# Moving two statistics chains ahead of the weight reloads in GpSimd's program

## The reference

```python
xn = layernorm(x)                       # over the last axis, eps 1e-5
a  = tanh(xn @ Wa.T + ba)               # (8, 4096, 64)
b  = tanh(xn @ Wb.T + bb)
h[t] = a[t] * h[t-1] + b[t]             # scan over the 4096 tokens
attn = xn + h @ Wout.T + bout
scale = mean(abs(weight))               # weight is 2048 x 2048
w_t = clip(round(weight / (scale + 1e-10)), -1, 1)
ffn = xn @ (w_t * scale).T + bias
y = x + attn + ffn
```

## Time and profile before

| what | us |
|---|---|
| median of the timed runs (758.03 to 758.31) | 758.17 |
| the profiled execution's own time | 758.21 |
| span of its slowest core (core 0) | 756.6 |
| spans of its eight cores | 752.0 to 756.6 |
| mean granted TensorE clock of the cores | 0.992 to 0.995 |

### The profile page before, as it was taken

One profiled execution on the slowest core, in us unless ns is written; L12 is line 12 of the kernel. 1 busy time (PEld: TensorE's weight loads), 2 busy tenths in 40 slices (PEclk: granted clock), 3 DMA queues, 4 the chain that ended last, 5 costly groups with the idle time before them and its releaser, 6 DMA issues.

```text
span 756.6 us, 11239 instructions; the slowest of 8 cores (752.0 to 756.6 us)
## 1 busy us (share of the span) xinstructions
PE 586.7 (78%) x3740; PEld 310.8 (41%) x3804; DVE 349.0 (46%) x303; ACT 235.7 (31%) x250; POOL 217.3 (29%) x742
## 2 busy tenths in 40 slices
PE   0111314404799999999999999999999999999995
PEld 0110213303444454444444454444444444544442
DVE  0000099841354455544556545555445555455521
ACT  0664414504422332233222223322332222232220
POOL 0000012265033333333333334333333333333410
PEclk9999999999899999999999999999999999999998
DMA  7998128840132233233433333333343333233222
GB/s 228 340 331 270 28 106 252 263 158 1 56 112 112 112 112 112 112 131 121 160 146 113 112 112 112 112 112 113 128 161 137 131 112 113 112 112 112 112 84 83
DMA packets 16831, 103.02 MB, mean 136 GB/s; under 512 B 4326, under 2 KB 4358, under 8 KB 4358
## 3 DMA queue, kind: packets, MB, share of 16 engines
q1 hardware_dynamic: 9350, 51.96, 21.2%
q0 software_dynamic: 7424, 50.34, 17.4%
HBM read 68.73 MB, written 33.55 MB: 135 GB/s over the span
## 4 chain that ended last, share of the span: by engine, by line
PE 64%; DMA 10%; ACT 8%; issue 4%; ACTq 4%; DVEq 4%; DVE 3%; POOL 1%; POOLq 1%; SPq 1%
PE pffn L560 15%; PE pffn L546 15%; PE pffn L556 14%; PE pffn L543 13%; DMA vv<-wf 8%; ACT xnT L302 4%; ACTq L301 3%; PE pab L534 2%; PE ptr L570 2%; DVE wbn L368 2%; DVEq L362 2%; ACT xnT L298 1%; DVEq L367 1%; DMA outb<-wf 1%; POOL wocv L612 1%
## 5 line engine op out<-in xcount | busy, mean ns | idle before, releaser
L560 PE MATMUL pffn<-w_rhs,xnT 128*128 128x512 bf16 x512 | 195.1, 381 | 3.3 <-ACT w_rhs L259 1.7
L546 PE MATMUL pffn<-w_rhs,xnT 128*128 128x512 bf16 x496 | 188.0, 379 | 1.6
L556 PE MATMUL pffn<-w_rhs,xnT 128*128 128x512 bf16 x480 | 182.9, 381 | 0.0
L543 PE MATMUL pffn<-w_rhs,xnT 128*128 128x512 bf16 x465 | 176.2, 379 | 0.0
L346 DVE TENSOR_REDUCE sums<-sx 128x1 f32<-128x2048 f32 x32 | 73.2, 2286 | 140.4 <-DMA sx<-x 140.1
L298 ACT COPY xnT<-ptr 128x1024 bf16<-128x1024 bf16 x31 | 31.4, 1012 | 243.2 <-PE ptr L570 243.2
L397 DVE SCALAR_TENSOR_TENSOR outb<-pffn,negs,vv 128x1024 f32<-128x1024 f32 x32 | 41.1, 1284 | 117.7 <-PE pffn L586 102.5
L280 ACT ACTIVATE xnb<-sx,nmr,yr 128x2048 bf16<-128x2048 f32 x31 | 65.0, 2096 | 96.3 <-POOLq L657 96.2
L623 POOL TENSOR_SCALAR mm_<-sums 128x1 f32<-128x1 f32 x32 | 7.2, 226 | 249.9 <-DVE sqscr L348 246.8
L480 PE MATMUL ptr<-sidn,wbn 128*128 128x128 bf16 x256 | 28.5, 296 | 65.1 <-DVE wbn L368 37.6
L556 PEld LDWEIGHTS pffn<-w_rhs,xnT 128*128 128x128 bf16 x512 | 50.3, 98 | 62.5 <-issue 2.9
(11 more groups left out here) (109 smaller groups left out, 607.3 us busy)
## 6 DMA issues: line engine op xcount, KB each, us to landing
sx<-x SPq DMA_DIRECT2D x32, 1024.0 KB, 5.2
y<-outb POOLq DMA_DIRECT2D x32, 1024.0 KB, 5.7
outb<-wf POOLq DMA_DIRECT2D x11, 1024.0 KB, 7.3
wtile<-wf SPq DMA_DIRECT2D x8, 1024.0 KB, 11.0
vv<-wf SPq DMA_DIRECT2D x8, 1024.0 KB, 13.8
sqscr<-wf POOLq DMA_DIRECT2D x5, 1024.0 KB, 6.4
wasb<-wa SPq DMA_DIRECT2D x1, 512.0 KB
wosb<-wout SPq DMA_DIRECT2D x1, 512.0 KB, 18.1
```

Of the source, the lines that this page charges most:

```text
L543: tensor.matmul(pffn[:, 0:512], lhs, w_rhs[:, 2048 * c:2048 * c + 512], start=st_, stop=False)
L546: tensor.matmul(pffn[:, 512:1024], lhs, w_rhs[:, 2048 * c + 512:2048 * c + 1024], start=st_, stop=False)
L556: tensor.matmul(pffn[:, 1024:1536], lhs, w_rhs[:, 2048 * c + 1024:2048 * c + 1536], start=st_, stop=False)
L560: ins = tensor.matmul(pffn[:, 1536:2048], lhs, w_rhs[:, 2048 * c + 1536:2048 * c + 2048], start=st_, stop=False)
```

## The change

Only the order in POOL's program changes. The sixteen weight reloads and the sixteen wocv DMAs, which stood ahead of `chain(0)` and `chain(1)`, now stand behind both, directly ahead of POOL's loop over the token tiles. No instruction is added, removed or altered, and no other engine's program changes.

```diff
             g.memset(two_i[:, :], 2)
-            for j in range(NW):
-                if j < 3:
-                    g.wait_ge(s_wabs, 10 + 2 * j)
-                    if j == 2:
-                        g.wait_ge(s_sums, 2)
-                else:
-                    g.wait_ge(s_tern, j - 2)
-                sl = j % 3
-                buf = outb if sl < 2 else sqscr
-                so = (sl % 2) * D if sl < 2 else 0
-                g.dma_start(out=buf[:, so:so + D],
-                            in_=wf_d[128 * j:128 * (j + 1), :]
-                            ).then_inc(s_wlb[sl], 16)
-            g.wait_ge(s_cvecv, 1)
-            for i in range(16):
-                g.dma_start(out=wocv[64:65, 128 * i:128 * (i + 1)],
-                            in_=cneg[i:i + 1, :]).then_inc(s_cvr, 16)
-
             def chain(j):
...
             chain(0)
             chain(1)
+            for j in range(NW):
+                if j < 3:
+                    g.wait_ge(s_wabs, 10 + 2 * j)
+                    if j == 2:
+                        g.wait_ge(s_sums, 2)
+                else:
+                    g.wait_ge(s_tern, j - 2)
...
+            g.wait_ge(s_cvecv, 1)
+            for i in range(16):
...
             for k in range(NT):
```

More of the change, by code:

```diff
@@ L660, in _ @@
             chain(1)
+            for j in range(NW):
[5 more added lines that the diff above has]
+                    g.wait_ge(s_tern, j - 2)
+                sl = j % 3
+                buf = outb if sl < 2 else sqscr
+                so = (sl % 2) * D if sl < 2 else 0
+                g.dma_start(out=buf[:, so:so + D],
+                            in_=wf_d[128 * j:128 * (j + 1), :]
+                            ).then_inc(s_wlb[sl], 16)
+            g.wait_ge(s_cvecv, 1)
+            for i in range(16):
+                g.dma_start(out=wocv[64:65, 128 * i:128 * (i + 1)],
+                            in_=cneg[i:i + 1, :]).then_inc(s_cvr, 16)
             for k in range(NT):
```

## The result

The changed kernel takes 747.08 us (median of 7 runs, 746.51 to 749.34); the kernel before, timed with it, 758.0 (6 runs). The ratio is 0.986, with a 95% interval of 0.9847 to 0.9873: 10.9 us less. The forecast was 748.3 us, 9.9 us less.

A forecast was written before the change was run, and what follows sets the result against it. TensorE's steady loop is full and untouched, so the some 200 us of preparation before it decide; -6.2 (first read) and -3.7 (ternary stage to TensorE, late start included) make -9.9, 748.3 us; range 743.5 to 754.

The forecast's parts named there:

- Term 1: First read of the weight: without two early reloads in the full DMA engines, the last Abs comes 6.2 us earlier.
- Term 2: Start of the ternary stage: reloads issued behind both chains put the first comparison 19.6 us later, at 123.26.
- Term 3: First comparison to TensorE: twelve tiles keep 48.04 us, xnb fits between copies, tile 12's copies end 3.7 us earlier.
- A: Ternary stage: squaring doesn't hold POOL (-1.95) and twelve tiles take 45.7 us: -14.2, 744.0 us; chance 0.15.
- B: First three queued reloads share the queue, the first landing 12.7 us after issue instead of 6.5: 754.5 us; chance 0.17.
- C: Ternary stage bound by its three buffers' round trip; landing of 10.3 us eats the gain, 12.9 gives 768 us; chance 0.04.

The follow-up runs named there:

- run 1: The kernel before, with weight reloads 0 and 1 held back until ScalarE has cast the second small weight: 751.29 us, ratio 0.9919.
- run 7: The changed kernel, with reloads 1 and 2 each issued only when the one before has landed: 752.14 us, ratio 0.9937 to the kernel before.
- Run 4: The changed kernel, with VectorE's sums of tiles 0 and 1 heading its program and reloads 0 and 1 awaiting the second small weight's cast: 717.61 us, ratio 0.9476.
- run 3: The changed kernel, with only chain(0) ahead of the reloads and chain(1) behind the wocv DMAs: 739.74 us, ratio 0.977 to the kernel before.
- run 5: The kernel before, with reloads 0 and 1 held back, VectorE's sums at its program's head, chains still behind all reloads: 740.73 us, ratio 0.9786.
- run 2: The kernel before, with both chains moved behind reloads 0 and 1 but ahead of the other reloads: 751.69 us profiled, 753.6 in a second execution.

## Why the prediction was right

**Term 1, the first read (-6.2 us).** Right in cause and near in size: at the last Abs core 5 measured -6.8 us, the eight cores -4.6 to -7.9 with a mean of -6.4, and run 1 alone -6.1 us in the total. One step behind it was off: what follows the last Abs isn't quite a fixed sequence. The second small weight was waited for longer, and of the 6.8 us only 5.9 reached VectorE's sums.

**Term 2, the late start of the ternary stage (+19.6 us on the old clock).** Measured on core 5: the first comparison moved from 103.05 to 118.09, and with the 5.9 us by which the sums came earlier taken out that is +20.9 us. Piece by piece: semaphore to chain 0.26 us (0.56 taken), chain to chain 9.28 (7.45 + 1.95 = 9.40), chain(1) from 102.06 to 109.34 is 7.28 (7.12), to the issue 0.76 (0.70), to the comparison 7.99 us (6.5). The hold of 1.95 us, the one cost that no row had shown, was 1.86 (L620 took 2.05 us; beside an idle VectorE it takes 0.19). The one piece that was off is the landing, too short by 1.5 us on the core that became the slowest, too long by 1.1 us on the even ones. Together the pieces make +1.3 us, which is the difference to 19.6.

**Term 3, from there to TensorE.** Twelve tiles were taken at the old pace, 48.04 us on core 0. On core 5 they went from 47.87 to 46.59, which made up for the landing, but this is luck of that core: on core 0 they went from 48.04 to 48.79, and over the eight cores the mean was 47.4 before and 47.3 after. The old pace was the right one to take. The copies of tile 12 ended at 171.89 where 172 was written down. That xnb would lie between copies at no cost is in the rows above: the copies of tile 11 come late, those of tile 12 (idle 1.16 us before them) on time. From the thirteenth comparison to that end it was 7.21 us, as in the sum (3.71 + 3.50). The wocv issues took 9.5 us from 169.88 and delayed nothing that the distances behind tile 12 show.

**The sum.** -9.9 us forecast, -10.9 measured by the medians, -9.8 in the span of core 5. At the copies of tile 12 core 5 gained 9.5 us: 0.4 us less of term 1 at the sums and 1.3 us more of term 2 than forecast stood against 1.3 us less for the tiles. The mechanism was right; that the total was hit so closely owes something to errors that cancel. Core 0, whose rows the forecast used, gained 12.7 us (756.6 to 743.9), 2.8 more than forecast, and its trace says where: its sums of tile 0 end at 90.51 instead of 98.98, 2.3 us more than term 1 gave; the landing was 5.38 us, 1.1 less than taken; the small pieces of term 2 gave 0.2, and the tiles took 0.8 back. The spans of the eight cores fell by 8.9 to 12.9 us. These are single executions, and a core's span moves between executions by more than that difference (core 0 of the changed kernel: 740.1 to 746.1), so the forecast is to be held against the time of the slowest core alone.

**The rivals.** A, the cheaper head, was wrong in both halves: the squaring does hold POOL, and the tiles kept their old pace (46.4 to 48.8 us for twelve, where VectorE's own 3.81 us would make 45.7). B, reloads that share so that the first lands with the third, was refuted: it would have meant over 12 us to the first comparison where 5.4 to 8.0 were seen, but on odd cores some delay of that kind exists (run 7). C, the slow side, asked for landings above 10.3 us in the loop; in the loop of the changed kernel they took 5.4 to 9.2 over all cores, and VectorE waited 0.33 and 0.59 us at the tiles shown and at most tiles not at all.

**What it left out.** The forecast rightly said that a 24 us wait would go and that only 10 us would come of it. It didn't say that the missing part was a matter of place. Run 4, with sums, chains and reloads in other places, is 29 us faster than the changed kernel. Of these, 7 us are chain(1) (run 3). The 10 us for the sums on VectorE (run 5 against run 1) stood on the path of the kernel before as well, so they are a second prize beside the first. How the rest divides into chain(0), its hold, and the reloads' exposed issue and landing, no run shows.

## What to carry to other kernels

When one engine's in-order program feeds two consumers, ask for each block not only who waits for it, but what the block behind it then loses: here 24 us of waiting left and 20 us of late start came in its place. A prefetch far ahead of its use isn't free while another queue is fighting for the same DMA engines; hold it back until the urgent stream is through. And of the places tried here for the small statistics the best was neither directly before nor behind the transfers, but where their input lands and both engines are idle: with the reloads held back as well, that was worth 5.2% against 1.4% for the reordering.

## What the runs showed of the hardware

Odd cores got their first reload later than even ones. In the changed kernel, with all eight cores issuing three at nearly the same time, the four odd cores took 7.2 to 8.0 us from issue to comparison and the four even ones 5.4 to 5.5. In run 7 the third reload shows it again: core 0 waits 2.72 us for it and core 5 waits 5.53. In run 3 it was 6.5 to 7.2 on the odd cores and 5.4 to 5.5 on cores 0, 2 and 6, but 6.4 on core 4, so the split isn't clean in every execution. Why it is there isn't settled by these runs.

The hold of POOL by VectorE is of two kinds. POOL's arithmetic is held by the comparison (one SBUF input, run 2: L624 and L629 took 1.25 and 1.22 us instead of 0.19) and by the squaring and wbn (two), and isn't by the reduction. A DMA issue on POOL is held by the comparison alone, as two stretches of the kernel before show for the wocv issues (durations min/median/max), first beside the wbn of 156.88, then beside the comparison of 159.32:

```profile
L612 POOL DMA_DIRECT2D wocv<-cneg x3: 511/512/518, 156.9 to 157.9; - x3
```

```profile
L612 POOL DMA_DIRECT2D wocv<-cneg x3: 494/522/1389, 158.8 to 160.7; - x3
```

Three issues took 0.51 to 0.52 us beside wbn; beside the comparison one took 1.39, as long as the comparison (1.29) and 0.1 more. The reload issues say the same: in the changed kernel, core 5, those at 122.38, 126.42 and 168.94 end 0.11 to 0.12 us behind the comparison beside them, whether that makes them 1.18, 1.35 or 0.94 us long. This fits the Trainium skill, page "SBUF — State Buffer", section "SBUF: two separate sides", which limits the hold by a two-input instruction to GpSimd work that reads SBUF. That a DMA issue reads none is shown by no run here.

POOL is slow to begin a chain behind its DMA issues: the chain that followed the sixteen wocv issues started after 2.82 us of idle time, 2.81 or 2.82 on every core of that run and 2.81 in run 3, where a chain behind a chain starts after 0.33. Between the last issue and the chain's first instruction the program has a wait that had long been met and a drain; that it is the drain is read from the program, not shown by a run.
